# An octonion feed-forward kernel: the copied and negated slots of the gate and up tables made by ScalarE instead of VectorE

## The reference, cut to what matters

```python
def reference(x, itok, cond_weights, w_gate, w_up, w_down):      # x: (32, 64, 1024)
    y = jnp.einsum('bct,bcd->bdt', x, cond_weights[itok])         # a 64x64 matrix per batch entry
    def oct_ternary_linear(xp, W):                                # W: (8, out/8, in/8)
        scale = jnp.mean(jnp.abs(W))
        Wq = scale * jnp.clip(jnp.round(W / scale), -1.0, 1.0)    # -1, 0 or 1 times scale
        M = jnp.einsum('jik,jod->koid', S_OCT, Wq)                # octonion signs
        return jnp.einsum('...id,koid->...ko', xp, M)
    gate = oct_ternary_linear(y.reshape(.., 8, 128), w_gate)      # 1024 -> 2728 (8 x 341)
    up   = oct_ternary_linear(y.reshape(.., 8, 128), w_up)
    h    = silu(gate) * up
    return x + oct_ternary_linear(h.reshape(.., 8, 341), w_down)
```

## Time and profile before

| | before |
|---|---|
| median of 3 runs | 708.36 us (706.26 to 708.71) |
| the profiled execution | 708.42 us |
| its span | 706.6 us |
| busy PE / PEld | 670.8 / 621.8 us |
| busy DVE / ACT / POOL | 529.0 / 326.6 / 360.0 us |
| granted PE clock, mean | 0.985 of full |

### The profile page before, as it was taken

The page is one execution under the profiler, slowest core; times in us unless marked ns, Lnnn a source line. Parts: engine busy times, 40 slices in busy tenths (PEclk is TensorE's granted clock), DMA queues, the critical chain, the costliest instruction groups (busy, mean ns, idle before and its releaser), DMA issues.

```text
span 706.6 us, 17737 instructions
## 1 busy us (share of the span) xinstructions
PE 670.8 (95%) x7302; PEld 621.8 (88%) x7302; DVE 529.0 (75%) x897; ACT 326.6 (46%) x562; POOL 360.0 (51%) x411
## 2 busy tenths in 40 slices
PE   3579989999999999999999999999999999999987
PEld 3468889899999999999999999999999999988986
DVE  1897956868877688767877688866878688777884
ACT  4554665255443546254453545245452554434430
POOL 1200468347636566348556466367654366365553
PEclk9899999999999999999999999999999999999996
DMA  8100003032002200032001210032000200020001
GB/s 330 64 2 1 1 2 125 7 115 64 2 2 89 95 2 2 1 121 64 2 2 53 96 38 1 2 121 65 1 2 24 98 1 2 2 90 32 1 2 60
DMA packets 10579, 31.55 MB, mean 45 GB/s; under 512 B 3330, under 2 KB 3330, under 8 KB 10370
## 3 DMA queue, kind: packets, MB, share of 16 engines
q1 hardware_dynamic: 9906, 28.81, 11.7%
q10 hardware_dynamic: 592, 1.61, 0.7%
HBM read 22.02 MB, written 8.39 MB: 43 GB/s over the span
## 4 chain that ended last, share of the span: by engine, by line
PE 80%; DVE 9%; issue 4%; ACT 3%; POOL 1%; DMA 1%; ACTq 0%; DVEq 0%; POOLq 0%
PE ps L1154 40%; PE ps L1310 22%; PE ps L1162 9%; PE ps L1141 4%; PE ps L1214 3%; DVE z_op L910 1%; DVE pu_sb L801 1%; DVE pu_sb L965 1%; DVE pu_sb L932 1%; PE ps L1148 1%; DMA cond_bd<-in_L_cond_weights_dram 1%; ACT z_op L697 1%; POOL z_f L592 1%; POOL h_pairs L592 1%; ACT down_c L783 1%
## 5 line engine op out<-in xcount | busy, mean ns | idle before, releaser
L592 POOL TENSOR_TENSOR h_pairs<-h_f 128x256 f32<-128x256 f32 (+2 forms) x128 | 135.0, 1082 | 197.9 <-ACT h_f L683 138.8
L1154 PE MATMUL ps<-y_op,gate_table 128*128 128x256 f16 x1408 | 182.5, 275 | 7.0 <-DVE y_op L894 4.2
L1154 PE MATMUL ps<-y_op,up_table 128*128 128x256 f16 x1408 | 179.9, 273 | 0.2 <-DVE up_table L846 0.2
L1154 PEld LDWEIGHTS ps<-y_op,gate_table 128*128 128x128 f16 x1408 | 138.6, 99 | 24.4 <-DVE y_op L894 4.3
L1154 PEld LDWEIGHTS ps<-y_op,up_table 128*128 128x128 f16 x1408 | 137.7, 98 | 16.6 <-DVE up_table L846 0.7
L503 POOL TENSOR_TENSOR o_sb<-o_sb,wd_sb 128x256 f32<-128x256 f32 (+1 forms) x150 | 87.3, 619 | 91.0 <-DVE wd_sb L1026 89.8
L592 POOL TENSOR_TENSOR z_f<-h_pairs 128x512 f32<-128x512 f32 (+1 forms) x80 | 102.8, 1305 | 33.3 <-DVE z_op L910 31.0
L1162 PE MATMUL ps<-third_table,y_op 128*128 128x170 f16 x1408 | 108.3, 236 | 0.0
L1162 PEld LDWEIGHTS ps<-third_table,y_op 128*128 128x128 f16 x1408 | 104.7, 97 | 0.3
L801 DVE TENSOR_TENSOR pu_sb<-ps,q_sb 128x170 f32<-128x170 f32 (+1 forms) x128 | 65.0, 508 | 39.9 <-ACT q_sb L714 17.6
L1310 PE MATMUL ps<-down_u,z_op 128*128 128x256 f16 (+1 forms) x768 | 93.0, 278 | 1.9 <-DVE z_op L910 1.8
(11 more groups left out here) (98 smaller groups left out, 669.6 us busy)
## 6 DMA issues: line engine op xcount, KB each, us to landing
x_in<-in_x_dram SPq DMA_DIRECT2D x8, 1024.0 KB, 5.2
o_sb<-in_x_dram SPq DMA_DIRECT2D x16, 512.0 KB, 3.5
out_dram<-o_sb SPq DMA_DIRECT2D x15, 512.0 KB, 2.7
h_op<-in_L_ffn_w_gate_dram ACTq DMA_DIRECT2D x3, 512.0 KB, 6.6
h_op<-in_L_ffn_w_up_dram SPq DMA_DIRECT2D x3, 512.0 KB, 7.0
z_op<-in_L_ffn_w_down_dram SPq DMA_DIRECT2D x1, 1536.0 KB, 11.0
out_dram<-o_sb SPq DMA_DIRECT2D x2, 256.0 KB, 3.4
cond_bd<-in_L_cond_weights_dram SPq DMA_DIRECT2D x30, 16.0 KB, 3.0
```

Source lines behind the costliest of these rows:

```text
L592: return pool.tensor_tensor(dst, a, b, ALU.add if sign > 0 else ALU.subtract)
L1154: mm = pe.matmul(dst, table[m][:, slot, q, :], y_op[:, op, e, :], start=(i == 0 and e == 0), stop=(i == len(terms) - 1 and e == 1))
```

## The change

The four `tensor_scalar` instructions leave DVE's `build_table`, which now raises `slots_built` four times per window. ACT makes the same slots in a new function `copy_slots`, with its own semaphores `slots_copied`. It is called for gate window 0 inside `y_hi(0)`, ahead of the third piece; for up window 0 behind the sum over the down weights, just before chunk 0; and for the other four in ACT's `chunk`, in the chunk after the one of `TABLE_AFTER`, behind `split_h` and ahead of what `first_tile_at` does. PE and ACT wait for both semaphores where they waited for one; POOL waits for the sums alone.

```diff
@@ -213,7 +213,8 @@
     slots = {w: n for n, w in enumerate(order)}
     assert set(slots) == {w[0] for w in [*wr.values(), *wpr.values()]} | set(wq.values())
     NSLOT = len(slots)
-    NBUILD = 8
+
+    NBUILD, NCOPY = 4, 4
 
     xr = x.rearrange("b c t -> (b c) t")
     outr = out.rearrange("b c t -> (b c) t")
@@ -392,6 +393,7 @@
         compared = sem("compared")
         tern_ready = [sem("gate_tern_ready"), sem("up_tern_ready"), sem("down_tern_ready")]
         slots_built = [sem("gate_slots_built"), sem("up_slots_built")]
+        slots_copied = [sem("gate_slots_copied"), sem("up_slots_copied")]
         down_mixed = sem("down_mixed")
         down_c_ready = sem("down_c_ready")
         down_u_ready = sem("down_u_ready")
@@ -518,6 +520,9 @@
             eng.dma_start(cond_bd[C * h:C * h + C, b // 2, C * h:C * h + C],
                           cond_w[bass.ds(which, 1), :, :].rearrange("a c d -> (a c) d")).then_inc(cond_loaded, 16)
 
+        def slots_at(m, w, a, n):
+            return third_table[:, a:a + n, m, :] if w == THIRD else table[m][:, a:a + n, w, :]
+
         block = ctx.enter_context(nc.Block())
 
         @block.sync
@@ -642,6 +647,18 @@
 
         @block.scalar
         def _(act):
+            def copy_slots(m, w):
+
+
+                t, copied = tern[m][w][:, :, 0:ROWS[w]], slots_copied[m]
+                act.wait_ge(tern_ready[m], w + 1)
+                act.activation(slots_at(m, w, 18, 2), t[:, 4:8:3], ACT.Copy).then_inc(copied, 1)
+                act.activation(slots_at(m, w, 20, 1), t[:, 4:5], ACT.Copy, scale=-1.0).then_inc(copied, 1)
+                act.wait_ge(slots_built[m], NBUILD * w + 2)
+                for n in range(2):
+                    act.activation(slots_at(m, w, 8 + 3 * n, 3), slots_at(m, w, 1 + 4 * n, 3), ACT.Copy, scale=-1.0
+                                   ).then_inc(copied, 1)
+
             def copy_y(T, r):
                 act.wait_ge(y_done, 4 * T + r + 1)
                 if T > 0:
@@ -658,6 +675,8 @@
                     act.wait_ge(up_done, NC * T)
                 for i, ops in enumerate(Y_PIECES):
                     if i == NY - 1:
+                        if T == 0:
+                            copy_slots(0, 0)
                         act.wait_ge(y_summed, 5 * T + 5)
                     act.activation(y_op[:, ops, 0, :], y_f[:, ops], ACT.Copy, scale=y_up(T)
                                    ).then_inc(y_hi_ready, 1)
@@ -692,6 +711,7 @@
 
                     for m in range(2):
                         act.wait_ge(slots_built[m], NBUILD * min(NQ, k + 2))
+                        act.wait_ge(slots_copied[m], NCOPY * min(NQ, k + 2))
                     if k > 0:
                         act.wait_ge(tern_ready[2], NQ)
                 act.activation(z_op[0:ROWS[k // 2], k, 0], z_of(k), ACT.Copy).then_inc(z_hi_ready, 1)
@@ -714,6 +734,8 @@
                         act.activation(q_sb[:], bank_q, ACT.Copy).then_inc(q_copied, 1)
                 if 0 < c <= C3:
                     split_h(T, c - 1)
+                if T == 0 and c - 1 in TABLE_AFTER:
+                    copy_slots(*TABLE_AFTER[c - 1])
                 if T == 0:
                     first_tile_at(c, 0)
                 act.wait_ge(g_ready, n + 1)
@@ -770,6 +792,7 @@
             y_hi(0)
             act.wait_ge(down_loaded, 16)
             sum_abs(2 * NQ - 1, raw_down_at, NQ * raw_n, abs_sum[2])
+            copy_slots(1, 0)
 
             corr_list = [(w, item) for w in range(NQ) for item in corr.items()]
             per_chunk = -(-len(corr_list) // len(CORR_AFTER))
@@ -830,20 +853,11 @@
             def build_table(m, w):
 
                 t, built = tern[m][w][:, :, 0:ROWS[w]], slots_built[m]
-
-                def to(a, n):
-                    return third_table[:, a:a + n, m, :] if w == THIRD else table[m][:, a:a + n, w, :]
-
                 dve.wait_ge(tern_ready[m], w + 1)
-                signed_add(to(0, 4), t[:, 0:4], t[:, 4:8], 1).then_inc(built, 1)
-                signed_add(to(4, 4), t[:, 0:4], t[:, 4:8], -1).then_inc(built, 1)
-                signed_add(to(14, 2), t[:, 4:7:2], t[:, 1:8:6], 1).then_inc(built, 1)
-                signed_add(to(16, 2), t[:, 4:7:2], t[:, 1:8:6], -1).then_inc(built, 1)
-                dve.tensor_scalar(to(18, 2), t[:, 4:8:3], 1.0, None, ALU.mult).then_inc(built, 1)
-                dve.tensor_scalar(to(20, 1), t[:, 4:5], -1.0, None, ALU.mult).then_inc(built, 1)
-                dve.wait_ge(built, NBUILD * w + 2)
-                dve.tensor_scalar(to(8, 3), to(1, 3), -1.0, None, ALU.mult).then_inc(built, 1)
-                dve.tensor_scalar(to(11, 3), to(5, 3), -1.0, None, ALU.mult).then_inc(built, 1)
+                signed_add(slots_at(m, w, 0, 4), t[:, 0:4], t[:, 4:8], 1).then_inc(built, 1)
+                signed_add(slots_at(m, w, 4, 4), t[:, 0:4], t[:, 4:8], -1).then_inc(built, 1)
+                signed_add(slots_at(m, w, 14, 2), t[:, 4:7:2], t[:, 1:8:6], 1).then_inc(built, 1)
+                signed_add(slots_at(m, w, 16, 2), t[:, 4:7:2], t[:, 1:8:6], -1).then_inc(built, 1)
 
             def scales_of_tile(T):
 
@@ -1169,6 +1183,7 @@
                 if T == 0 and c == C3:
                     for m in range(2):
                         pe.wait_ge(slots_built[m], NBUILD * NQ)
+                        pe.wait_ge(slots_copied[m], NCOPY * NQ)
                 if c % 2 == 0:
                     pe.wait_ge(q_copied, u)
                     for s in range(SUB):
@@ -1251,6 +1266,7 @@
                             pe.wait_ge(u_ready, n - 1)
                     if T == 0 and c % 4 == 0:
                         pe.wait_ge(slots_built[m], NBUILD * (q + 1))
+                        pe.wait_ge(slots_copied[m], NCOPY * (q + 1))
                     for h in range(2):
                         mm = group(bank_r(s, m)[:, h], m, [(slots[wr[h, K, p][0]], q, wr[h, K, p][1])
                                                            for p in range(4)])
@@ -1270,6 +1286,7 @@
                 if T == 0 and c % 4 == 0:
                     for m in range(2):
                         pe.wait_ge(slots_built[m], NBUILD * (c // 4 + 1))
+                        pe.wait_ge(slots_copied[m], NCOPY * (c // 4 + 1))
                 if c % 2 == 0:
                     shared_pair(T, c)
                 shared(T, c)
```

## The result

| | before | changed |
|---|---|---|
| median | 706.26 us (17 runs, 704.06 to 708.71) | 703.87 us (17 runs, 702.76 to 705.19) |
| the profiled execution | 708.42 us | 704.86 us |
| its span | 706.6 us | 703.0 us |
| busy PE / DVE / ACT | 670.8 / 529.0 / 326.6 us | 668.4 / 526.0 / 334.0 us |

The ratio is 0.9966, with a 95% interval of 0.9954 to 0.9977: 2.4 us faster, a third of a percent. Of the 3.3 us between the forecast 707.2 and 703.87, 2.1 are the starting point: 17 runs put the kernel before at 706.26 us, its first three at 708.36. The other 1.2 us are gain that the forecast did not have.

The account below looks back on a forecast made before the run. TensorE was taken to bound the kernel, with only first-tile stalls affected. Terms 0 + 0 - 0.63 + 0 + 0 - 0.52 = -1.15 us took 708.36 us to 707.2 us, range 705.2 to 709.2.

Parts of the forecast that it names:

- the first two tables: Gate's and up's first windows in the first tile: ScalarE's copies are covered or end in time, 0 each.
- up's second: Up's second window: TensorE waits for ScalarE's square of a y round, so VectorE's gain adds 0.
- gate's second: Gate's second window: VectorE's saving goes straight through to TensorE's idle before chunk 2's own products, -0.63 us.
- POOL's earlier start: Up's third window: POOL's z rounds start 1.15 us earlier, shortening VectorE's comparison of the last down window, -0.52 us more.
- up's first window: Tightest place: TensorE's up products start at 30.6 behind ScalarE's last copy, against 30.62 before; 0.0, bounds -0.15 to +0.5.
- the shift is kept, and the steady tiles keep it to the end: After the first tile's tables: engines start each other by turns, so the -1.15 us lasts to the kernel's end.
- The second rival: Chunk 3, 52 to 54 us: TensorE's clock doesn't fall, saving 1.8 us more; -2.95 us, 705.4; chance 0.12.
- The first: Rival: POOL's earlier start gives nothing at the last down window's comparison; -0.63 us, 707.7; chance 0.22.
- second term: The -0.52 us at the last down window's comparison, from POOL's z rounds starting earlier.
- The third: Rival: VectorE's time saved on all six tables counts in full, -3.56 us, 704.8; chance 0.04.
- The fifth: Rival: another wait ends at the same time at 42.93 or 30.6, so no gain, 708.4; chance 0.10.
- The fourth: Rival: ScalarE is late with up's first table; with copies twice as dear +2.05 us, 710.4; chance 0.10.

Follow-up runs that it names:

- the filled pair: Kernel before and changed kernel, each with unread products in TensorE's four longest idle times: 703.79 and 702.61 us.
- the four filled profiles: Profiles of the kernel before, the changed kernel and two kernels with y rounds moved, all with unread products in TensorE's idle times: 703.79, 702.61, 701.05, 701.17 us.
- after + 10: Changed kernel with ten more products on TensorE in chunk 4 of the fourth tile: 706.39 us, 0.9994.
- POOL late: Changed kernel, but POOL's z rounds also wait for ScalarE's last copy of the last table: 705.50 us, one execution.
- y rounds moved with up on VectorE: Changed kernel with the third and fourth y rounds moved back and up's first two windows made by VectorE again: 703.95 us, 0.9956.
- Experiment 4: Ten products in the fourth tile added to the changed kernel, 706.39 us, or removed from the kernel before, 704.28 us.
- experiment 7: Unread products filling TensorE's longest idle times: kernel before 703.79, changed 702.61, y rounds moved 701.05, the same with up's first two windows on VectorE 701.17 us.
- experiment 3: Changed kernel with POOL also waiting for ScalarE's last copy, 705.50 us, or with gate's second window made by VectorE, 706.03 us; one execution each.

## Why the prediction was wrong, point by point

**The terms of the sum were right.** Nothing at the first two tables and at up's second, 0.62 us at gate's second (0.63), 0.5 us by POOL's earlier start (0.52): 1.12 to 1.14 us by the profiles and 1.18 us by the filled pair, against 1.15. ScalarE's copies cost what the line between two rows gave. At up's first window TensorE waited 0.51 us for ScalarE instead of 0.22 for VectorE, but the gate products before it ended 0.26 us earlier against their own start, since the clock rose sooner there.

**The step that failed is "the shift is kept, and the steady tiles keep it to the end".** The shift was kept through the steady tiles (1.56 us of lead at 687.08), but it was not neutral behind them: the forecast put the last tile at nothing. There TensorE idles 1.84 us and the clock falls. What this costs has two values, in the 13 unfilled profiles of all kernels here. From the restart to TensorE's end it takes (the fall read from windows of half a microsecond):

| | from the restart to TensorE's end | the clock falls behind the restart by |
|---|---|---|
| the four filled profiles | 9.0 us | it doesn't |
| nine profiles, the changed kernel's two among them | 12.3 us | 0.7 to 1.9 us |
| four: the kernel before (708.42 us), after + 10, POOL late, y rounds moved with up on VectorE | 14.0 us | 0.15 to 0.5 us |

At full clock the two groups of products take 3.67 and 5.53 us (the filled kernels). So a shift of a microsecond between the restart and the clock's fall is worth up to 1.6 us more. Experiment 4 shows that it moves the median by 1.2 us in either direction, and experiment 7 that with the clock kept up only the work is left. That it was this place that gave the change its 1.2 us is an inference from there: the shift is the same, 1.1 us. The mean clock of its 25 runs doesn't prove it, since it can't tell the places apart (0.988 in a profile with the long stretch at the end, 0.985 in one with the short). The changed kernel isn't free of the long stretch either: with one wait added (POOL late, +0.5 us) it had it.

**The second rival named the clock, but at one place and as all or nothing.** It looked only at the fall in chunk 3 and asked whether its idle changes length. That fall is real and comes and goes: with the same idle of 2.2 us it is in seven of the eleven unfilled profiles that have the y rounds at their old place, in both of the changed kernel's and in one of two of the kernel before. Without it the first tile's down products start 1.7 us earlier (79.38 us behind gate's first products and 81.07 in the two profiles of the kernel before; 1.8 by the rival). A third place is the start: the low stretch there lasts 10.2 us instead of 6.8 in four profiles and costs 0.6 to 1.0 us before chunk 2. The last tile, where the chain is TensorE's too and the page's clock row shows a 6 in its last slice, was not read. The right rival would have been: the change moves all that follows by 1 us, so any low stretch behind it can be met differently, by up to some 2 us either way.

**The starting point was the larger miss, 2.1 of 3.3 us.** The sum was made against a profiled run of 708.42 us, and the three runs seemed to agree with it (706.26 to 708.71). The kernel's own 17 runs spread over 4.65 us, in groups near 704.5, 706.6 and 708, four times the effect forecast. Measured from 706.26 us the forecast would have been 705.1, so that the range was too narrow for the starting point alone.

**The rivals.** The first (no second term) is refuted by experiment 3. The third (VectorE's time in full, 704.8 us) comes nearest to the measured time, and only by chance: by the trace 1.1 of its 3.56 us reached TensorE. The fifth (another wait takes over) is refuted by the idle of 0.87 us and by experiment 3. The fourth (ScalarE late) has its place right and its point of decision open: at a cost of 1.04 us there the time did not rise, because the clock did not fall in chunk 3. Whether the clock's falls at the start, in chunk 3 and at the end are tied to each other, and why the kernel's runs fall into groups, is not settled. The changed kernel's runs form two groups as well, 702.8 to 703.9 and 704.5 to 705.2 us; both of its profiles are of the second.

## What to carry to other kernels

When a change is worth less than the spread of the kernel's own runs, read TensorE's granted clock slice by slice before trusting a sum of work: a shift of a microsecond can be doubled or cancelled at the next low stretch, and the trace tells where, the run's mean clock only that it happens. To price such a change, keep the clock up with products that nobody reads and compare that pair; here it gave 1.18 us (known to some 0.7) for 1.15 us of predicted work, and the fillers themselves took 3 us off. The sharpest reading is neither: match the two traces place by place from a common point ahead of the change. Work moved off a full engine pays only where that engine's result is what is waited for; here two of six tables paid, and one of them through a third engine.

## What the runs showed of the hardware

Ten products (1.09 us) added or removed in mid-kernel moved the time by 2.3 us; 1.04 us of real delay at the start moved it by 0.1 to 0.4. An idle of 1.84 us in the last tile was followed by a fall of the granted clock to 1.2 GHz in all 13 unfilled profiles, and in none of the four where products filled it. The fall cost TensorE 3.3 us when it came 0.7 to 1.9 us behind the restart and 5.0 us when it came within 0.5 us of it. VectorE's comparison of 1024 columns took 0.75, 1.02 or 1.53 to 1.59 us, according to how much of POOL's operation it had to sit out, and its two copies of 255 columns took 0.89 us beside POOL instead of 0.40. ScalarE's f16 copies and negatives between table slots took 0.30 us for 128 columns, 0.41 to 0.43 for 256 and 0.51 to 0.53 for 384, as the line between two of its other copies (0.305 us for 128 columns, 1.053 for 1024) gives.
